# The last two groups of a decoder kernel: gelu transposed tile by tile, down-projection in fp32, the end of the schedule reordered

## What is computed

```
q = x Wq + bq ; k = x Wk + bk ; v = x Wv + bv          # 16 heads of 64
q' = exp(q wq_feat) ; k' = exp(k wk_feat)               # 32 features a head
out = (q' (k'^T v)) / (q' . sum(k') + 1e-6)
x = norm(x + out Wproj + bproj)
Q = x WQ^T + b ; K, V = ctx WK^T + b, ctx WV^T + b      # 16 heads of 8
x = norm(x + softmax(Q K^T / sqrt 8) V Wo^T + bo)
h = gelu(x T(W_fc)^T)                                   # T: weights to -1, 0, 1
h = norm(h) * ln_w + ln_b                               # over 512
x = norm(x + h T(W_proj)^T)
```

## Time and profile before

| | |
|---|---|
| median of three runs | 682.11 us |
| the profiled execution | 683.16 us, span 681.4 us |
| TensorE busy | 655.5 us (96%) |
| VectorE, ScalarE, GpSimd busy | 538.5, 440.6, 453.6 us |
| mean granted clock of TensorE | 0.983 |

### The profile page before, as it was taken

One profiled execution on the slowest core, in us unless ns is written; L12 is line 12 of the kernel. 1 busy time (PEld: TensorE's weight loads), 2 busy tenths in 40 slices (PEclk: granted clock), 3 DMA queues, 4 the chain that ended last, 5 costly groups with the idle time before them and its releaser, 6 DMA issues.

```text
span 681.4 us, 30517 instructions
## 1 busy us (share of the span) xinstructions
PE 655.5 (96%) x13176; PEld 460.9 (68%) x13176; DVE 538.5 (79%) x1483; ACT 440.6 (65%) x757; POOL 453.6 (67%) x501
## 2 busy tenths in 40 slices
PE   9999999999999999999999999999999999999765
PEld 6776777766766767666776776676776676666553
DVE  1656678888888888888788888798888889696787
ACT  3536565849477584948668494948758496867342
POOL 3133234877769586777859687777959678867353
PEclk9999999999999999999999999999999999998779
DMA  8101122342632644263443535363353524331310
GB/s 329 34 18 33 36 49 51 46 98 57 96 74 49 112 57 94 55 109 56 61 116 49 96 55 107 50 103 73 58 114 54 97 49 81 68 62 41 72 33 32
DMA packets 119849, 49.79 MB, mean 73 GB/s; under 512 B 110497, under 2 KB 110626, under 8 KB 119586
## 3 DMA queue, kind: packets, MB, share of 16 engines
q1 hardware_dynamic: 119714, 47.83, 35.9%
HBM read 16.88 MB, written 4.19 MB: 31 GB/s over the span
## 4 chain that ended last, share of the span: by engine, by line
PE 79%; POOL 8%; DVE 4%; DMA 4%; issue 3%; SPq 1%; ACT 0%; POOLq 0%; DVEq 0%
PE bank L329 15%; PE bank L319 7%; PE bank L346 7%; PE bank L441 4%; PE bank L399 4%; PE bank L426 4%; DMA gT<-gs 2%; PE bank L312 2%; PE bank L494 2%; PE bank L269 2%; PE bank L342 2%; PE bank L286 2%; PE bank L271 2%; PE bank L270 2%; PE bank L277 2%
## 5 line engine op out<-in xcount | busy, mean ns | idle before, releaser
L329 PE MATMUL bank<-Mh,GT 128*32 128x128 f32 x4096 | 127.4, 274 | 0.9 <-issue 0.8
L329 PEld LDWEIGHTS bank<-Mh,GT 128*32 128x32 f32 x4096 | 111.4, 110 | 24.8 <-issue 18.3
L874 DVE TENSOR_REDUCE mx<-bank 128x8 f32<-128x512 f32 x128 | 78.1, 682 | 12.7 <-PE bank L399 12.7
L1055 POOL TENSOR_TENSOR gall<-gall,lnr 128x512 f32<-128x512 f32 x56 | 71.1, 1281 | 18.2 <-DVE st L844 18.2
L825 DVE COPY GT<-bank 128x512 f32<-128x512 f32 x77 | 50.4, 687 | 35.2 <-PE bank L329 19.6
L645 ACT ACTIVATE PT<-bank 128x512 f32<-128x512 f32 x128 | 64.7, 621 | 17.1 <-PE bank L426 17.0
L1013 POOL TENSOR_TENSOR rstd<-ve,mhalf 128x4 f32<-128x4 f32 x64 | 66.6, 1041 | 5.3
L346 PE MATMUL bank<-Cb,qT 128*64 128x128 f32 x1024 | 67.2, 273 | 0.0
L1060 POOL TENSOR_TENSOR gs<-gall,gs 128x512 f16<-128x512 f32 x56 | 64.1, 1163 | 3.8 <-ACT gs L688 3.8
L319 PE MATMUL bank<-kp,xs 64*128 64x512 f32 x256 | 64.0, 616 | 0.0
L831 DVE COPY Cb<-bank 128x512 f32<-128x512 f32 x80 | 52.5, 671 | 8.4 <-PE bank L329 8.2
(11 more groups left out here) (187 smaller groups left out, 1679.3 us busy)
## 6 DMA issues: line engine op xcount, KB each, us to landing
xT<-in_xT SPq DMA_DIRECT2D x16, 256.0 KB, 2.9
xs<-in_x_nat SPq DMA_DIRECT2D x16, 256.0 KB, 3.6
cxT<-in_cxT SPq DMA_DIRECT2D x16, 256.0 KB, 3.6
out_y<-yo SPq DMA_DIRECT2D x16, 256.0 KB, 2.0
Qm<-in_Wvp SPq DMA_DIRECT2D x1, 1024.0 KB, 7.5
gT<-gs SPq DMA_TRANSPOSE x56, 3.4
gall<-in_Wff SPq DMA_DIRECT2D x1, 768.0 KB, 10.1
small<-in_small SPq DMA_DIRECT2D x1, 523.0 KB, 8.7
```

The costliest lines, as they stand in the source:

```text
L329: m = e.matmul(bk[32 * j:32 * j + 32, tile(g_)], GT[b % 4][:, tile(hh, 32)], Mh[:, tile(hh)], start=True, stop=True)
L874: e.tensor_reduce(mx[s % 2][:, c0:c0 + 8], bank[uses["score", s, i][0]][:, :].rearrange("p (n k) -> p n k", k=64), AX.X, ALU.max).then_inc ...
L1055: e.tensor_tensor(g[t][:, :], g[t][:, :], lnr[:, :], ALU.mult).then_inc(s_gs, 1)
```

## The change

Constants and the lists. In HEAD only `wk` and `wb` change places. TAIL is written anew:

```diff
-WIDE = {"score": 4, "prob": 4, "mh": 2}
+WIDE = {"score": 4, "prob": 4, "flip3": 2, "mh": 2}
-FILL = {("wb", 0, 0): 8, ("wk", 0, 0): 8, ("oturn", 14, 1): 11, ("down", 15, 0): 16}
+FILL = {("wk", 0, 0): 25, ("rows", 15, 0): 2}
 HEAD = """
-wb wk wq k0@0 ...
+wk wb wq k0@0 ...
 TAIL = """
...
-proj1@3 st2@3 down1@4 rows@2 g4+@1 g5+@1 g6@1 ap2@3 g7+@1 c4@1 dT@1 c5@1 c6@1 down2@4 prob0@2 st3@5 bc0@1 bc1@1 bc2@1 bc3@1 ab2@3 c7@1 gs0@3 up0@3
-down3@4 up1@3 stat@3 ap3@5 up2@3 up3@3 kproj@1 o0@1 o1@1 o2@1 o3@1 st1@1 st3@4 vproj@1 pv0+@2 gs1@3 gh0@3 prob1@2 ap1@1 gs2@3 cs0@2 flip@1 oturn0@2
-gl0@3 qproj@1 pv1+@2 oturn1@2 score0@1 score1@1 down0@3 gh1@3 proj0@2 gl1@3 gl2@3 down1@3 gh2@3 cs1@2 gh3@3 gs3@3 rows@1 down2@3 proj1@2 gl3@3 prob0@1
-prob1@1 st2@2 ap2@2 ap3@4 ab2@2 down3@3 st3@3 flip3@2 pv0+@1 pv1@1 oturn0@1 up0@2 ab1@1 cs0@1 up1@2 oturn1@1 cs1@1 stat@2 ap3@3 up2@2 up3@2 proj0@1
-proj1@1 st2@1 turn0@2 turn1@2 turn2@2 ap2@1 turn3@2 flip3@1 down0@2 down1@2 down2@2 ab2@1 down3@2 st3@2 up0@1 up1@1 stat@1 up2@1 up3@1 turn0@1 turn1@1
-turn2@1 turn3@1 ap3@2 down0@1 down1@1 down2@1 down3@1 st3@1 ap3@1
+down0@4 gl3@4 kproj@1 proj1@3 st2@3 rows@2 st3@5 ap2@3 down1@4 g6+@1 g7+@1 c4+@1 dT@1 c5+@1 c6+@1 down2@4 ab2@3 down3@4 gs0@3 prob0@2 bc0@1 bc1@1 bc2@1
+bc3@1 c7@1 up0@3 up1@3 up2@3 gs1@3 stat@3 up3@3 o0@1 o1@1 prob1@2 ap3@5 o2@1 o3@1 st1@1 st3@4 gh0@3 pv0+@2 pv1+@2 gs2@3 ap1@1 gl0@3 gl1@3 oturn0@2
+gs3@3 flip+@1 oturn1@2 gh1@3 qproj@1 cs0@2 score0@1 gh2@3 tw@1 gl2@3 score1@1 gh3@3 proj0@2 down0@3 cs1@2 down1@3 gl3@3 rows@1 down2@3 proj1@2 st2@2
+vproj@1 prob0@1 ab1@1 ap3@4 down3@3 st3@3 ab2@2 prob1@1 ap2@2 pv0@1 flip3@2 ap3@3 oturn0@1 up0@2 up1@2 up2@2 up3@2 pv1+@1 stat@2 cturn0+@1 oturn1@1
+proj0@1 turn0+@2 turn1@2 cturn1+@1 turn2+@2 proj1@1 st2@1 turn3@2 down0@2 down1@2 ap2@1 down2@2 down3@2 flip3@1 up0@1 ab2@1 up1@1 st3@2 stat@1 up2@1
+turn0+@1 ap3@2 up3@1 turn1+@1 turn2+@1 turn3+@1 down0@1 down1@1 down2@1 down3@1 st3@1 ap3@1
```

TensorE's part. `cturn` is new (group 15), its results go to SBUF in fp32 by one copy; `turn` goes by tile; `down` of the groups 14 and 15 and `proj` of group 15 are fp32; `score` waits for Qu alone, and `prob` now has the wait for the whole of Qm:

```diff
-                w.wait_ge(*emptied("qproj", s))
+                w.wait_ge(s_qu, s + 1)
...
+            def cturn(s, tp):
+                bk, done = start("cturn", s, tp)
+                w.wait_ge(*emptied("oturn", s, tp))
+                for bb in two:
+                    m = e.transpose(bk[:, tile(bb)], cn[tp][:, tile(bb)], ident[:, :])
+                m.then_inc(done, 1)
...
+                if s in cross_by_pe:
+                    w.wait_ge(*emptied("cturn", s, tp))
+                    for bb in two:
+                        m = e.matmul(bk[:, tile(bb)], cT32[tp][:, tile(bb)], xWo[:, :], start=True, stop=True)
...
-            def turn(s, c):
-                bk, done = start("turn", s, c)
-                for t in range(4):
-                    w.wait_ge(*emptied("up", s, t))
-                    m = e.transpose(bk[:, tile(t)], g[t][:, tile(c)], ident[:, :])
+            def turn(s, t):
+                bk, done = start("turn", s, t)
+                w.wait_ge(*emptied("up", s, t))
+                for c in range(4):
+                    m = e.transpose(bk[:, tile(c)], g[t][:, tile(c)], ident[:, :])
...
                 if s in by_pe:
+                    w.wait_ge(s_tpw, 1)
+                    w.wait_ge(*emptied("turn", s, t))
                     for c in range(4):
-                        w.wait_ge(*emptied("turn", s, c))
+                        m = e.matmul(bk[:, 0:128], gT32[t][:, tile(c)], tpw[:, tile(c)], start=(c == 0), stop=(c == 3))
```

```diff
+            def last_down(s, t):
+                y = yo[s % 2][:, tile(t)]
+                w.wait_ge(s_mv["4"], 4 * s + 4)
+                w.wait_ge(*emptied("sbar", 0))
+                w.wait_ge(*filled("down", s, t))
+                e.scalar_tensor_tensor(y, Sneg, mv["4"][:, 2 * t:2 * t + 1], bank[uses["down", s, t][0]][:, 0:128],
+                                       ALU.mult, ALU.add).then_inc(emptied("down", s, t)[0], 1)
+                w.wait_ge(s_rstd["4"], s + 1)
+                w.wait_ge(s_x2b, s + 1)
+                w.wait_ge(*emptied("down", s, t))
+                e.scalar_tensor_tensor(y, y, rstd["4"][:, t:t + 1], x2[s % 2][:, tile(t)], ALU.mult, ALU.add).then_inc(s_ly, 1)
+                w.wait_ge(s_ly, t + 1)
+                e.bn_stats(st["3"][:, 6 * t:6 * t + 6], y).then_inc(s_st["3"], 1)
```

More of the change, by code:

```diff
@@ L25, in wait_ge @@
             self.value[sem.name] = value
[L28 to L31 removed]
+WIDE = {"score": 4, "prob": 4, "flip3": 2, "mh": 2}
+BANKED = "k q ks kst dT bc g c o flip kproj vproj qproj score rows prob pv oturn cturn proj flip3 up turn down wq wk wb mh biasA bias2 nbeta gam bias3 sbar".split()
+FILL = {("wk", 0, 0): 25, ("rows", 15, 0): 2}
 WHOLE = "small1 small2 x1s flip3 ab1 ab2 st1 st2 st3 ap1 ap2 ap3 bias2 bias3".split()
 HEAD = """
[L36 removed]
+wk wb wq k0@0 small1 k1@0 zeros WkT k2@0 WqT split@0 k3@0 q0@0 q1@0 ks@0 g0+@0 g1+@0 loadx@0 mh0 mh1 Wvp g2+@0 g3+@0 bv q2@0 small2 kst@0 Wff nbeta
 q3@0 gam biasA g4+@0 g5@0 split@1 xb@0 loadc@0 g6@0 g7@0 c0+@0 dT@0 c1+@0 loadx@1 loadx@2 c2+@0 c3@0 xw c4@0 c5+@0 c6@0 c7+@0 bias2 bc0@0 bc1@0 bc2@0
@@ L522, in pe_program @@
                     {"k": kexp, "q": qexp, "bc": broadcast, "g": gmat, "c": cmat, "o": outp, "score": score, "prob": prob, "pv": pv,
-                     "oturn": oturn, "proj": proj, "up": up, "turn": turn, "down": down}[name](s, t)
+                     "oturn": oturn, "cturn": cturn, "proj": proj, "up": up, "turn": turn, "down": down}[name](s, t)
         def act_program(e):
@@ L660, in flip3 @@
                     w.wait_ge(*filled("up", s - 1, 3))
-                w.wait_ge(*filled("flip3", s))
-                e.activation(x2T[:, 0:512], bank[uses["flip3", s, 0][0]][:, :], ACT.Copy).then_inc(s_x2hp, 1)
+                for h in two:
+                    w.wait_ge(*filled("flip3", s, h))
+                    e.activation(x2T[:, tile(h, 256)], bank[uses["flip3", s, h][0]][:, 0:256], ACT.Copy).then_inc(s_x2hp, 1)
             def up(s, t):
@@ L669, in up @@
                 elif s - 1 in by_pe:
-                    w.wait_ge(*filled("turn", s - 1, 3))
+                    w.wait_ge(*filled("turn", s - 1, t))
                 else:
@@ L673, in up, with cturn, turn @@
                 e.activation(g[t][:, :], bank[uses["up", s, t][0]][:, :], ACT.Gelu).then_inc(emptied("up", s, t)[0], 1)
-            def turn(s, c):
+            def cturn(s, tp):
                 if s > 0:
-                    w.wait_ge(*filled("down", s - 1, 3))
-                w.wait_ge(*filled("turn", s, c))
-                b3 = bank[uses["turn", s, c][0]][:, :].rearrange("p (t n) -> p t n", t=4)
-                e.activation(gTc[c][:, :, 0, :], b3, ACT.Copy, scale=lnw[:, c:c + 1]).then_inc(s_ghp, 1)
+                    w.wait_ge(*filled("proj", s - 1, tp))
+                copy("cturn", s, tp, cT32[tp][:, :], cols=256)
+            def turn(s, t):
+                if s > 0:
+                    w.wait_ge(*filled("down", s - 1, t))
+                copy("turn", s, t, gT32[t][:, :])
             def ghi(s, t):
@@ L899, in flip3 @@
                     w.wait_ge(*filled("up", s - 1, 3))
-                w.wait_ge(s_x2hp, by_pe.index(s) + 1)
-                e.tensor_tensor(x2T[:, 512:1024], bank[uses["flip3", s, 0][0]][:, :], x2T[:, 0:512], ALU.subtract).then_inc(emptied("flip3", s)[0], 1)
+                for h in two:
+                    w.wait_ge(s_x2hp, 2 * by_pe.index(s) + h + 1)
+                    e.tensor_tensor(x2T[:, tile(2 + h, 256)], bank[uses["flip3", s, h][0]][:, 0:256], x2T[:, tile(h, 256)],
+                                    ALU.subtract).then_inc(emptied("flip3", s, h)[0], 1)
             def stat(s):
@@ L938, in dve_program @@
                     {"ks": ksum, "flip": flip}[name](s)
-                elif not on_act and name in ("g", "c", "pv"):
-                    {"g": gmat, "c": cmat, "pv": pv}[name](s, t)
+                elif not on_act and name in ("g", "c", "pv", "cturn", "turn"):
+                    {"g": gmat, "c": cmat, "pv": pv, "cturn": cturn, "turn": turn}[name](s, t)
                 elif name == "qproj":
```

100 lines of the change are left out of this document (65 added, 35 removed).

## The result

The changed kernel takes 673.59 us (median of four runs, 672.83 to 675.15) against 681.72 us for the kernel before, measured with it; the ratio is 0.9874, 95% interval 0.9839 to 0.991. Run once more, unchanged, beside three other kernels, it took 670.86 us (0.9851, 0.9818 to 0.9884; the kernel before had 681.21 there). The forecast was 672.3, in a range of 667.5 to 679. The profiled execution took 673.73 us (span 671.9), the second one 669.95 (span 668.2).

The account below looks back on a forecast made before the run. Bounds: half-clock TensorE at the head, a full middle, group 15's single data path behind 618 us. Sum 3.0 - 0.5 + 0.3 + 2.4 + 0 + 3.4 + 1.2 = 9.8 us: 672.3 us, range 667.5 to 679.

Parts of the forecast that it names:

- the root 17 to 18 us behind prob: Sign at the end: root of group 15's second norm still 17 to 18 us behind prob, released by GpSimd or VectorE's statistics.
- Head: Start to q of group 0: one block of 25 fills raises the clock, so folds and k run faster; 3.0 us gained.
- Up to group 15's norm: Stretch before group 15's first norm: moved steps and filled waits against idle time; 0.5 us lost, bounds 1.3 lost, 0.8 gained.
- costs nothing, because GpSimd would hold the root anyhow: Before group 15's first norm: prob of group 14 placed between the o steps adds no time.
- Scores: Group 15's scores start with Qu; maxima start at Qu + 2.95 in place of Qu + 5.37; 2.4 us gained.
- I keep the 3.35 us: Group 15, from maxima to prob: time unchanged at 3.35 us, gain 0.
- The rival of the queue: SyncE's queue, down2 and proj1 ahead of prob take the scores' gain; late by 2.4 us, 674.7 us; chance 0.14.
- Prob to root: Prob to root of group 15's second norm: 17.7 us, gain 0, as GpSimd follows an unchanged ScalarE chain.
- More than counted: Rival: prob at full clock and the 0.8 of idle time give 3.5 us more, 668.8 us; chance 0.15.
- Root to gelu and gelu to end: Group 15's tail: gelu at root + 4.3, 3.4 us gained; last norm ends at gelu + 12.1, 1.2 gained.
- hidden behind the copies already: First gelu to end: the three products that GpSimd drops were already hidden behind the copies.
- Half clock in the fp32 downs: Rival at group 14's downs: half clock, 7.2 us a group; 675.2 us, or 679.5 if low to the end; chance 0.22.

Follow-up runs that it names:

- four profiles with the old order: Kernel before (681.72 us), and that kernel with the new head alone (681.25), all rewritten code in the old order (682.94), or the turned context alone (683.25).
- the new wait in the old order: All rewritten steps in the order, head and fills of the kernel before, group 15's context still turned by DMA: 682.94 us, ratio 0.9987.
- the old wait in the new order: Kernel after with scores waiting again for all of Qm: 675.29 us, ratio 0.9899.
- three kernels with rows early: Kernel after with group 15's v projection, group 14's second cs and rows ahead of group 13's downs; no fills 675.09 us, eight 675.43, two 674.66.
- the kernels without fills: Kernel after without the two fills ahead of rows, 673.31 us; the same with v projection, second cs and rows ahead of group 13's downs, 675.09 us.
- the new head: Kernel before with only the head changed, 25 fills ahead of wk and wb behind it: 681.25 us, ratio 0.9975.
- flip3 first: Kernel after with ap2 and flip3 of group 15 ahead of group 14's four downs: 679.69 us, ratio 0.9972.
- the eight: Kernel after with v projection, second cs and rows ahead of group 13's downs, eight fills ahead of group 14's DMA-fed projection: 675.43 us, ratio 0.9922.

## Why the prediction was right, and where it was not

**The total** came out at 673.6 (or 670.9) for 672.3, by steps most of which are seen in the rows, and with two errors of over 2 us that cancelled in the first profile. That it came within 1.3 us was luck to that extent. One of the signs that the prediction named, the root 17 to 18 us behind prob, did not come.

**Head**: 3.0 forecast, 2.8 in the profile pair, 2.45 on average. Right in mechanism. The earlier trace rows was one execution, and I took its half clock for the rule; one profile in four of the old head had full clock without the change.

**Up to group 15's norm**: 0.5 lost forecast, 1.97 measured. The unchanged code up to bc accounts for 0.57 of it and scatters between 547.7 and 553.1. The edited part, bc to norm, is steady: 57.25 to 57.87 in the four profiles with the old order, 58.28 to 59.59 in the ten with the new, 1.24 on average. The step that failed is that prob of group 14 between the o steps "costs nothing, because GpSimd would hold the root anyhow". With the old order the root follows GpSimd's product in all four profiles and the statistics wait 0.74 us for it; with the new one that hold is 0.08 to 0.33, and the statistics come 57.21 us behind bc on average, where they came at 55.37. The lists name the only step that TensorE now has ahead of the last o in addition, the second tile of that prob; it takes 1.22 us (614.34 to 615.56). What makes up the rest of the 1.84 is open, and the step was not moved back in a run of its own.

**Scores**: 2.4 forecast, 2.55 measured, maxima at Qu + 2.82 for 2.95. The mechanism stands (VectorE is the one waited for, and has no idle time between). But the three other profiles of the old order have 4.27 to 4.28, not the 5.37 of the earlier trace rows. In the execution of the earlier trace rows the granted clock was 0.50 from 625 to 628 (TensorE before):

```profile
624.18 1.56 PE L369 MATMUL bank<-x1T,small 128*128 128x512 f32 x2 [0.44 <-DVE x1T L782]
625.67 1.94 PE L441 MATMUL bank<-PT,Vblk 128*32 128x64 f32 x64
```

In the three others the clock stayed at 1.00 there, and these two pieces took 1.10 each and the eleven fills behind them 2.55 in place of 2.80. Behind Qu that is 0.84 at the second piece and 0.25 at the fills, together the 1.1. The change itself is worth 1.45; 1.1 was a dip of the clock in the one profile that I argued from. The 0.6 gained between norm and Qu is the same dip for 0.45, at the query projection (4.65 here, 4.19 to 4.20 in the other three). And the 1.45 needs wait and order together: the new wait in the old order has 4.28, the old wait in the new order 4.18.

**Maxima to prob**: "I keep the 3.35 us" failed in the first profile, by 2.2. The rival of the queue had the time (2.4) and not the place: it put the hold on SyncE's queue and on down2 and proj1 ahead of prob, and in this profile it was what stands ahead of rows on TensorE: proj0, fed by a late DMA, and two downs at half clock. In the three kernels with rows early it was on the queue. It is not steady: 0.3 in the second profile of the same code, 0.6 to 1.2 in the other kernels with the same list here and the fills kept.

**Prob to root**: 0 forecast, 2.4 gained. My reason was that ScalarE's chain from prob to gelu had "the same members in the same order". It had not. Before, a copy of OT and two of cs stood in it among the gelus; and prob ran at half clock, so that its exps ended at prob + 6.58. After, they end at prob + 5.41 (643.67) and the last of group 14's gelus at prob + 9.35 (647.61), where it was at prob + 11.99: 1.2 us by the clock and 1.5 by the copies. GpSimd still follows that chain, and the root of group 15 follows GpSimd and VectorE's statistics, which end within 0.03 us of each other. So the pace-setter that I named is right, and the constancy that I gave it is not. In the new list, where downs stand between the two tiles of prob, half clock would cost still more: the kernels without fills, or with them in vain, have 17.6 to 17.7 in place of 15.35. "More than counted" among the rivals had this clock in its price of 3.5, and it is the part of that rival that came; the two terms that the rival names add up to 2.3 (twice 0.77 and 0.8), not to 3.5.

**Root to gelu and gelu to end**: 3.4 and 1.2 forecast, 3.5 and 1.45 measured; both to 0.1 us the same in every kernel that keeps the order. The single row from which I priced the fp32 downs (0.11 an instruction) was enough. The kernel before is less steady: its unchanged tail behind the new head has 18.34 and 6.77 for prob to root to gelu, where this profile has 17.73 and 7.71, so up to 0.9 of the 3.5 hangs on the execution. And what I called the real relief at the end, the single copy, isn't enough by itself: with it and GpSimd's products the stretch has 13.52. That the products were "hidden behind the copies already" was the wrong step there; leaving the products out is what the gain needs.

**The rivals.** Half clock in the fp32 downs had 0.22 and is false: the clock is 1.00 from 640 to 665 in the kernel after. Its condition was right, though: where TensorE waits ahead of them (3.04 us with flip3 first, the DMA in the old order) the downs take 5.37 and 4.75. The Trainium skill ("TensorE: Matmul & The Clock Gate", part 4) has transpositions not count as busy for the clock. Here sixteen turns and four transpositions of context, with fp32 matmuls among them, stood between 647 and 652, and the clock was 1.00 in each stretch from there to 665 (two of the stretches are shown above). So in this kernel the turns among other work did not take it down; in the two others the fall came behind idle time of TensorE. No run here has transpositions alone.

**What is left open**: why the transposing DMA of cT is used 2.6 us after its issue in five profiles and 4.2 to 4.45 in five others, with the same list on both sides; whether the two fills are what keeps prob at full clock; what spreads the unchanged middle over 5 us; and whether the kernel after is faster than the three with rows early (670.86 against 674.7 to 675.4), when the middle of the kernel after was 0.8 to 3.0 us shorter in the profiles by nothing that the order explains. None of the experiments beats the kernel after.

## What to carry to other kernels

An order written by hand is worth what it fills: the rewritten steps in the old order gained nothing, one step moved ahead of the downs cost 4.3 us, since the idle time that it opened came with a fall of the clock. When a member of the critical chain is taken off one engine, list the same chain on each of the others anew, the order of a DMA queue included, before calling it unchanged. And before pricing a stall from one profile, look at the granted clock under it: 1.1 us of the stall at the scores was a dip of the clock in one execution, and the same prob cost 1.07 us a tile in some kernels and 1.96 in others that differ in two fills.

## What the runs showed of the hardware that I had not expected

- Under fp32 matmuls and transpositions, mixed densely, the clock stayed at 1.00 (650 to 655: TensorE busy 4.85 of 5 us).
- Two fills of 512 columns right ahead of rows went with full clock in prob in all seven profiles that have them, with the downs ahead of them or behind; none, or eight ahead of the DMA-fed projection instead, went with half clock (with the eight, 0.50 from 636 to 642). Since the clock's fall came before the fills in six of the seven, this is a count of seven against three and not a cause shown.
- From the start of M's issue to prob is 2.47 to 2.50 us in fourteen profiles, while a transposing DMA of group 14's context was used 2.6 us (five profiles) or 4.2 to 4.45 us (five) after the start of its issue, with nothing in between.
